# Forming the gate's rows inside the middle pass instead of ahead of the experts, and a loop for masked attention

## The reference, cut to what matters

```python
x = x + _L0_attn_ref(_layernorm(x), ...)          # self-attention, 16 heads
x = x + _L0_xattn_ref(_layernorm(x), ctx, ctx, ...)   # cross-attention, 64 keys a sequence
x = x + _L0_ffn_ref(_layernorm(x), ...)           # two matrices a sequence, no nonlinearity
x = x + _L1_attn_ref(_layernorm(x), ...)          # 8 experts, top 2 of a gate
x = x + _L1_xattn_ref(_layernorm(x), ctx, ctx, mask, ...)  # masked cross-attention
x = x + _L1_ffn_ref(_layernorm(x), ...)           # quantised feed-forward
# in _L1_attn_ref, the gate:
xn = rmsnorm(xf, gate_norm_w, 1e-6)
xn = rmsnorm(xn, norm_w, 1e-8)                    # inside bitlinear
xq = act_quant(xn)      # round(x * 127 / max|x| of the row) * max|x| / 127
wq = weight_quant(w)    # -1, 0 or 1, times mean|w|
gate_logits = xq @ wq.T # 4096 tokens x 8 experts
probs = softmax(gate_logits); topw, topi = top_k(probs, 2)
# then each expert takes the first 512 tokens that chose it
```

## Time and profile before

| | us |
|---|---|
| median of 3 runs (2372.21 to 2380.17) | 2373.59 |
| the profiled execution | 2368.86 |
| its span, first to last instruction | 2367.1 |
| span: load and self-attention | 1097.8 |
| span: middle, early part and loop | 272.3 |
| span: gate's rows and logits | 113.1 |
| span: routing, then scatter | 21.3 and 98.5 |
| span: experts | 220.0 |
| span: masked attention and the start of the last block | 382.0 |

### The profile page before, as it was taken

How to read it: one execution, slowest core, us unless ns; L and a number is a source line. 1 busy time by engine, 2 the same in 40 slices (tenths; PEclk the granted TensorE clock), 3 DMA queues, 4 the chain that set the end, 5 groups by cost and what they waited for, 6 DMA issues and landing times. The chain is left out here.

```text
span 2367.1 us, 42843 instructions
## 1 busy us (share of the span) xinstructions
PE 1715.8 (72%) x13321; PEld 1084.2 (46%) x13338; DVE 1550.3 (65%) x3111; ACT 1394.6 (59%) x2215; POOL 788.3 (33%) x749
## 2 busy tenths in 40 slices
PE   3789998989999898985888802122443788888577
PEld 1455555555555555553666601121222355555323
DVE  6877777777777777775233386744774675755775
ACT  3889888898979898991444412443553332323745
POOL 0534545454545455450000050470001444443000
PEclk9999999999999999996789955555766787878699
DMA  5222222222222222222122111332102201111001
GB/s 180 61 53 62 59 55 64 61 53 62 62 50 64 59 64 53 64 46 97 36 72 72 36 76 53 122 109 89 54 27 70 81 25 30 23 32 18 1 10 63
DMA packets 173822, 140.04 MB, mean 59 GB/s; under 512 B 83794, under 2 KB 155399, under 8 KB 173366
## 3 DMA queue, kind: packets, MB, share of 16 engines
q1 hardware_dynamic: 166710, 122.78, 19.4%
q0 software_dynamic: 6912, 14.71, 2.7%
HBM read 61.92 MB, written 20.97 MB: 35 GB/s over the span
## 5 line engine op out<-in xcount | busy, mean ns | idle before, releaser
L577 ACT ACTIVATE a_p_hi<-ps,a_probs_up,a_s_scale 128x512 f16<-128x512 f32 x512 | 397.7, 777 | 54.9 <-ACTq L575 54.1
L689 DVE TENSOR_REDUCE a_top<-ps 128x2 f32<-128x1024 f32 x256 | 313.1, 1223 | 132.6 <-DVEq L688 132.6
L578 ACT ACTIVATE a_probs<-ps,a_probs_up,a_s_scale 128x512 f32<-128x512 f32 x512 | 398.5, 778 | 0.0
L917 POOL TENSOR_TENSOR a_p_lo<-a_probs,a_p_hi 128x1024 f16<-128x1024 f32 x128 | 277.8, 2170 | 210.4 <-POOLq L916 169.1
L905 POOL TENSOR_TENSOR a_ops<-a_ident_down,a_top 64x256 f16<-64x256 f32 x256 | 158.9, 621 | 340.8 <-POOLq L900 332.3
L698 DVE TENSOR_TENSOR a_p_lo<-a_probs,a_p_hi 128x1024 f16<-128x1024 f32 x128 | 182.7, 1427 | 41.2 <-DVEq L697 41.2
L441 PE MATMUL ps<-a_ops 128*128 128x512 f16 x512 | 195.8, 382 | 17.7 <-PEq L439 17.6
L460 PE MATMUL ps<-a_v_hi,a_p_hi 128*128 128x65 f16 x2048 | 205.6, 197 | 2.1 <-PEq L455 2.0
L463 PE MATMUL ps<-a_v_lo,a_p_hi 128*128 128x64 f16 x2048 | 205.6, 195 | 0.0
L464 PE MATMUL ps<-a_v_hi,a_p_lo 128*128 128x65 f16 x2048 | 205.5, 196 | 0.0
L460 PEld LDWEIGHTS ps<-a_v_hi,a_p_hi 128*128 128x128 f16 x2048 | 191.2, 99 | 23.0 <-issue 11.1
(11 more groups left out here) (487 smaller groups left out, 3767.3 us busy)
## 6 DMA issues: line engine op xcount, KB each, us to landing
a_ops<-a_qk SPq DMA_DIRECT2D x384, 128.0 KB, 2.3
f_w<-in_L_ffn_W_dram SPq DMA_DIRECT2D x16, 1024.0 KB, 7.6
a_qd<-a_qk SPq DMA_DIRECT2D x128, 64.0 KB, 2.2
g_a<-in_L_attn_gp_w_dram SPq DMA_DIRECT2D x8, 1024.0 KB
X<-in_x_dram SPq DMA_DIRECT2D x8, 512.0 KB, 9.9
expert_in<-g_w SPq DMA_DIRECT2D x8, 512.0 KB
g_a<-in_L_attn_dp_w_dram SPq DMA_DIRECT2D x8, 512.0 KB
e_x_in<-expert_in SPq DMA_DIRECT2D x8, 512.0 KB, 4.3
```

The costliest lines, as they stand in the source:

```text
L577: nc.scalar.activation(p_hi[:, h % 2, k, :], scores, ACT.Exp, bias=probs_up[:], scale=s_scale[:])
L578: nc.scalar.activation(probs[:, h % 2, k, :], scores, ACT.Exp, bias=probs_up[:], scale=s_scale[:]).then_inc(st_taken, 1)
L689: nc.vector.tensor_reduce(top[:, c % 2, 2 * pair:2 * pair + 2], ps[:, ROW:ROW + 2, :], AX.X, ALU.max).then_inc(row_taken, 1)
L917: nc.gpsimd.tensor_tensor(p_lo[:, h % 2, 2:KT, :], probs[:, h % 2, 2:KT, :], p_hi[:, h % 2, 2:KT, :], ALU.subtract).then_inc(p_made_pool, 1)
```

## The change

The gate moves into the middle block. Its work on a sequence is cut into steps which follow the sequence's last addition by a fixed number of passes (NORMS 1, ROWS 2, SQUARES 3, QUANTISE 4, GATES 5), so the loop runs over b = 0..12. The small aggregates, inverse roots, `v`, `a`, `peak` stay on VectorE, but for four tiles at a time; the Newton steps go to GpSimd, except for the last sequence. `u` goes from GpSimd to ScalarE as one activation with a scale and a shift; the rounding to `r` goes from VectorE to ScalarE. The gate's weights are loaded and rounded in the early part of middle. Two `f_rows` are moved ahead of `scores` on TensorE, and ahead of the last two `w2_out` on ScalarE. The experts' first block begins with the softmax; its staging memory for weights is a tile of its own, so the loads no longer wait. In masked_attention the seven written-out passes become a hardware loop.

```diff
-        for b in range(B + 1):
+        for b in range(B + GATE_STEPS):
             if b < B:
                 in_order += [("pT", b), ("w2T", b, 0), ("w2T", b, 1)]
+            if 1 <= b <= B:
+                in_order += [("f_rows", b - 1, 0), ("f_rows", b - 1, 1)]
+            if 0 <= b - GATES < B:
+                in_order += [("gates", b - GATES)]
             if b + 1 < B:
                 in_order += [("scores", b + 1)]
...
+            if 0 <= b - QUANTISE < B:
+                in_order += [("gate_rows", b - QUANTISE)]
...
+                def newton(root, half, tmp, ready, done):
+                    pool.wait_ge(ready, 1)
+                    pool.sem_inc(ready, -1)
+                    for _ in range(3):
+                        nc.gpsimd.tensor_tensor(tmp, root, root, ALU.mult)
+                        pool.drain()
+                        nc.gpsimd.tensor_tensor(tmp, tmp, half, ALU.mult)
+                        pool.drain()
+                        nc.gpsimd.tensor_scalar(tmp, tmp, 1.5, None, ALU.add)
+                        pool.drain()
+                        nc.gpsimd.tensor_tensor(root, tmp, root, ALU.mult)
+                        pool.drain()
+                    pool.drain().then_inc(done, 1)
...
+                    if 0 <= b - SQUARES < LAST:
+                        newton(again_root[:], again_half[:], again_tmp[:], seeded_again, rooted_again)
+                    if 0 <= b - NORMS < LAST:
+                        newton(first_root[:], first_half[:], first_tmp[:], seeded, rooted)
...
+                def experts_rows(b):
+                    act.wait_ge(u_ready, 1)
+                    act.sem_inc(u_ready, -1)
+                    for t in range(TT):
+                        n = b * TT + t
+                        nc.scalar.activation(gate.u[:, n, :], X[:, n, :], ACT.Identity, scale=u_factor[:, t:t + 1], bias=u_shift[:, t:t + 1])
+                    act.wait_ge(v_made, 1)
+                    act.sem_inc(v_made, -1)
+                    for t in range(TT):
+                        nc.scalar.activation(g_junk[:, t * D:(t + 1) * D], g_v[:, t, :], ACT.Square, accum_out=squares[:, t:t + 1])
+                    act.drain().then_inc(squared, 1)
...
+                    for t in range(TT):
+                        nc.scalar.activation(a[:, t, :], a[:, t, :], ACT.Identity, scale=per[:, b % 2, t:t + 1], bias=up[:])
+                    act.drain()
+                    nc.scalar.activation(g_r[:].rearrange("p t d -> p (t d)"), a.rearrange("p t d -> p (t d)"), ACT.Identity,
+                                         bias=minus_up[:])
...
+                    if 0 <= b - GATES < B:
+                        gate_logits(b - GATES)
+                    if 0 <= b - SQUARES < B:
+                        gate_squares(b - SQUARES)
+                    if 0 <= b - ROWS < B:
+                        gate_values(b - ROWS)
+                    if 1 <= b <= B:
                         add_outputs(b - 1)
+                    if 0 <= b - NORMS < B:
+                        gate_norms(b - NORMS)
+                    if 0 <= b - SQUARES < B:
+                        gate_steps(b - SQUARES)
...
-                for b in range(B - 1):
+                with pe.Fori(0, B - 1) as b:
                     sequence(b, more=True)
```

More of the change, by code:

```diff
@@ L1275, in turn_back, with gate_rows, gates @@
                     last.then_inc(back_full, 1)
+                def gate_rows(b):
+                    bank = bank_of["gate_rows", b]
+                    pe.wait_ge(r_made, 1)
+                    pe.sem_inc(r_made, -1)
+                    take(bank)
+                    for t in range(TT):
+                        for c in range(DC):
+                            at = (t * DC + c) * P
+                            last = nc.tensor.transpose(ps16(bank)[:, at:at + P], g_r[:, t, c * P:(c + 1) * P], ident16[:])
+                    last.then_inc(r_turned, 1)
+                def gates(b):
+                    bank = bank_of["gates", b]
+                    pe.wait_ge(r_out, 1)
+                    pe.sem_inc(r_out, -1)
+                    take(bank)
+                    for t in range(TT):
+                        for c in range(DC):
+                            last = nc.tensor.matmul(ps[:, bank, t * E:(t + 1) * E], g_rT[:, t, c, :], gwT[:, c, :],
+                                                    start=(c == 0), stop=(c == DC - 1))
+                    last.then_inc(gates_full, 1)
                 for bank in range(BANKS):
@@ L1289, in _ @@
                                     ident[0:B * DC, 0:B * DC]).then_inc(cols_full, 1)
+                pe.wait_ge(gw_part, 1)
+                pe.sem_inc(gw_part, -1)
+                take(early_bank["gw"])
+                nc.tensor.matmul(ps[:, early_bank["gw"], 0:1], ones[:], gw_sum[:], start=True, stop=True).then_inc(gw_total, 1)
                 over.turn(pe, peak[:])
@@ L1329, in _ @@
                 last.then_inc(pre_full, 1)
+                pe.wait_ge(gw_round, 1)
+                pe.sem_inc(gw_round, -1)
+                take(early_bank["gwT"])
+                for c in range(DC):
+                    last = nc.tensor.transpose(ps[:, early_bank["gwT"], c * E:(c + 1) * E], gw[:, c * P:(c + 1) * P], ident[0:E, 0:E])
+                last.then_inc(gw_turned, 1)
                 for c in range(DC):
@@ L1344, in _ @@
                         turn_w2(b, 1)
+                    if 1 <= b <= B:
+                        for c in range(DC):
+                            f_rows(b - 1, c)
+                    if 0 <= b - GATES < B:
+                        gates(b - GATES)
                     if b + 1 < B:
@@ new lines, in gate_logits @@
+                def gate_logits(b):
+                    bank, seq = bank_of["gates", b], slice(b * TT, (b + 1) * TT)
+                    dve.wait_ge(gates_full, 1)
+                    dve.sem_inc(gates_full, -1)
+                    nc.vector.scalar_tensor_tensor(out=gate.logits[:, seq, :], in0=ps[:, bank, 0:TT * E].rearrange("p (t e) -> p t e", e=E),
+                                                   scalar=gw_mean[:], in1=g_step[:, seq].unsqueeze(2).broadcast_to([P, TT, E]),
+                                                   op0=ALU.mult, op1=ALU.mult).then_inc(free[bank], 1)
@@ L2718, in _ @@
                 power(0)
-                for b in range(B - 1):
+                with act.Fori(0, B - 1) as b:
                     sequence(more=True)
@@ L2808, in _ @@
                 maximum(0, 1)
-                for b in range(B - 1):
+                with dve.Fori(0, B - 1) as b:
                     sequence(b, more=True)
```

393 lines of the change are left out of this document (199 added, 194 removed).

## The result

The changed kernel takes 2308.03 us, the median of 4 runs (2299.66 to 2309.09), against 2372.9 us (4 runs, 2361.68 to 2380.17). The ratio is 0.9723, 95% interval 0.9678 to 0.9768: 65 us less, where 53 were forecast (2321 us, range 2298 to 2352).

| stage | before | after | difference | forecast |
|---|---|---|---|---|
| start of middle to the first `f_both` of `pair_turned` 1 | 73.5 | 76.7 | +3.2 | +1 |
| from there to the end of the last `f_outT` | 194.8 | 222.5 | +27.7 | +21 |
| last `f_outT` to the softmax | 117.1 | 35.5 | -81.6 | -78 |
| softmax to scatter | 21.3 | 21.8 | +0.5 | 0 |
| scatter | 98.4 | 102.9 | +4.5 | 0 |

A forecast was written before the change was run, and what follows sets the result against it. A VectorE chain before the softmax and, in middle's loop, ScalarE's first half plus TensorE's second were taken as the bound; -110.5 + 21 + 32.5 + 1 + 3 = -53 us gave 2321 us, range 2298 to 2352.

The forecast's parts named there:

- Removed: 110.5: Between middle's end and the softmax: of 113.2 us of VectorE's chain, 2.7 remain, so 110.5 us go.
- +32.5: Tail after the last `f_outT`: ScalarE's roundings, copies and squares, then logits, take 36.4 us instead of 3.9.
- The loop: Middle's passes: ScalarE's added work, less the moved `w2_out`, plus a clock loss in pass 8, costs 21 us.
- the same clock loss then falls on `scores` rather than on `outputs`, and I count no second one: Passes 5 to 7: TensorE waits about 3 us at `gates`; the clock loss only moves, adding nothing.
- The early part: Start of middle: the gate's loads, one reduction and one matmul join a chain, costing 1 us.
- The scatter: GpSimd's 64 indirect DMAs after the routing: unchanged at about 98 us, the fills having landed.
- Masked attention: The seven passes as a loop: branches and address registers cost 3 us, within 0 to 8.
- The same instructions and waits: Masked attention as a loop: nothing changes but a branch and address registers per pass, 3 us in all.
- the one in which `outputs` runs at full clock: Middle's loop: ScalarE's half shortens or TensorE's full clock regains the loss, hiding the 21 us; 2300 us, chance 0.13.
- fetches in the masked loop: Masked attention: each pass stops at its branch for a fetch, 28 us in seven passes; 2346 us, chance 0.06.
- GpSimd slowing VectorE: Gate work in middle: GpSimd's newtons hold VectorE up, 70 us or more beyond the forecast; 2391 us, chance 0.04.
- a factor of 2.2, not 2.7: VectorE's pass in middle: stretching the gate's 10 us decides the time from a factor of about 2.7 on.

The follow-up runs named there:

- Experiment 4: The changed kernel with the gate's eight small matmuls moved behind the last two turns of `w2` on TensorE: 2298.1 us, ratio 0.968 to the kernel before.
- experiment 5: Traces compared after one 2.06 us wait (pass 1 of 24.1 or 32.0 us); also the kernel before with only `f_rows` moved early: 2364.87 us.
- `before_rows`: The kernel before with only the two `f_rows` moved ahead of `scores` on TensorE and the last two `w2_out` on ScalarE: 2364.87 us, ratio 0.9966.
- Experiments 1 to 3: Masked passes looped on all engines (2355.87 us), TensorE (2371.66) or VectorE (2351.57), or given memsets (2357.35, 2357.84), against the kernel before; changed kernel unlooped: 2310.54.
- experiment 6: The changed kernel with the gate's matmuls behind the last `w2` turns and `u` formed by GpSimd instead of ScalarE: 2280.63 us, ratio 0.9602.

## Why the prediction was right, and where it was not

**The gate's chain.** "Removed: 110.5" and the tail's "+32.5" make -78.0; measured -81.6. The 2.8 us from the logits to the softmax were forecast as 2.7. From the last `f_outT` to the logits' end it took 32.7 us, not 36.4: the copy and its waits are 2.5 us a sequence, not 2.9, a rounding 3.5 with its waits, not 3.7, and `gate_u` with the squares 3.9, not 4.4. That ScalarE is what the tail waits for holds.

**The loop.** Forecast +21, measured +27.7. Passes 3 and 4 cost 2.6 and 3.7 us (forecast 2.8), pass 7 3.7 (forecast 4), pass 8 6.5 (forecast 7). Passes 1 and 2 gained 3.4 and 2.8 us instead of 1.6. Passes 5 and 6 are what was off: +9.1 and +8.4 instead of +4. The step that failed is "the same clock loss then falls on `scores` rather than on `outputs`, and I count no second one". It fell on both, and on `w2` and the values, so that TensorE came 5.1 us late for `outputs` in pass 5. Experiment 4 shows it: with only the values behind the wait, passes 5 and 6 cost 3.9 and 4.7 us. My mistake was to price a wait by its length and not by what is queued behind it at half clock. The length tells little here: in pass 6 TensorE waited 1.62 us at `f_rows` and only 0.96 at `gates`, the clock fell all the same while `scores` ran (near 1329.3), and `outputs` came 3.7 us late.

**The early part.** Forecast +1, measured +3.2 in the profiled execution. In the seven kernels that have the changed early part it took 76.7 and 76.9 us in two executions and 72.8 to 73.1 in five, and before it was 73.5. The two long ones are those in which TensorE's clock stayed at half there (experiment 5). So the +3.2 goes with the clock, and the forecast term is too small to be seen beside it.

**The scatter.** Forecast unchanged, measured +4.5 (102.9 us). It did not wait for the fills: SP issued the last of them at 1440.2, and the scatter began at 1454.4. About half of the 4.5 is the execution that it is compared with: the seven kernels that have the scatter of the kernel before took 98.4 to 101.4 us, 100.1 in the mean, the seven with the changed one 100.7 to 103.3, 102.1 in the mean. GpSimd's indirect DMA takes 0.97 us alone and up to 2.95 beside a rounding of VectorE. GpSimd's timeline of the changed kernel, and VectorE's:

```profile
1461.33 0.97 POOL L2064 DMA_INDIRECT expert_in<-gate_u,m_slot  x1 [0.30 <-issue]
1462.61 2.04 POOL L2064 DMA_INDIRECT expert_in<-gate_u,m_slot  x1 [0.31 <-issue]
1464.95 2.90 POOL L2064 DMA_INDIRECT expert_in<-gate_u,m_slot  x1 [0.30 <-issue]
```

```profile
1462.51 1.95 DVE L2232 TENSOR_SCALAR g_stage<-g_stage,g_minus_half_w 128x2048 bf16<-128x2048 f32 x2
1464.65 3.55 DVE L2238 SCALAR_TENSOR_TENSOR g_w<-g_stage,g_half_w 128x2048 bf16<-128x2048 f32 x2 [0.19 <-DVEq L2236]
```

Each slow DMA (over 1.2 us) has such a partner in both kernels, but for the first of the changed one. Before, 16 of the 64 were slow and lost 16.3 us over 0.97 each; after, 17, and 21.3. The rounding is the same work (48.12 and 48.45 us in the stage); how the two sequences of instructions fall on each other would then set the loss. This is read from the traces and was not tried. The Trainium skill (GPSIMD Engine Reference, section Specifications) lists GpSimd's SBUF interfaces as shared with VectorE, with contention where a VectorE instruction has two SBUF inputs. The second rounding instruction (`g_w<-g_stage`) has two, and beside it the DMAs took 1.93 to 2.95 us, so the trace agrees; of a DMA's issue the section says nothing.

**Masked attention.** Forecast +3, measured -22.7. "The same instructions and waits" was true of the instructions, and the price of 3 us for branches was not found: with the loop on TensorE alone the stage took 376.5 us, against 374.2 and 376.2 written out (`before_rows`). With the loop on VectorE its first instruction after a wait for scores starts 0.11 to 0.15 us later. What failed is the silent step that equal instructions have equal durations. Experiments 1 to 3 show that a shift of 0.04 to 0.21 us on VectorE, by its loop or by a useless memset, takes away a clock drop of some 10 us in most passes. Why the clock falls at one phase and not at the other stays open. The loop is worth 15.5 us on the kernel before. How much of the changed kernel's gain is the loop's is not settled: with its passes written out its masked attention took 357.5 us, between the two lengths, and the whole could not be told from the changed kernel's.

The mismatches cancel in part: loop +7, early part +2, scatter +4.5 and two small ones on one side; masked attention 26, the tail 4 and the last block 2 on the other. That the whole came out so near is partly luck: without masked attention the profiled gain would be 47 us, where 56 were forecast for the rest, and the 23 us that brought it up come from a clock drop that the prediction did not know of. Of the rivals, the one in which `outputs` runs at full clock happened in passes 1 and 2; "fetches in the masked loop" did not. GpSimd slowing VectorE did not happen with the newtons, which touch 4 or 12 values (they took 4.3 and 5.4 us in pass 5, and the 32 instructions of `gate_v` 0.47 to 0.50 us each), and did with `u`, in experiment 6. One figure of that rival is wrong by its own terms: 9 + 10 us times the factor reaches a pass of 31 us at a factor of 2.2, not 2.7.

## What to carry to other kernels

Price a wait on TensorE by all that is queued behind it, at both clocks, and put small matmuls with a late input where little stands between them and the next wait. When a stage that the change hardly touches moves by per cents, compare the granted clock of one pass before looking for a cause in the code, and shift the stage by 0.1 us with a useless instruction to tell chance from cause. Work that leaves the engine which ends the waits can come back in full: `u` was 2.07 us a pass and a wait, and six passes gave 14 us. Where the work goes must be looked at too: in the tail it gave nothing.

## What the runs showed of the hardware that was not expected

The same code with the same 2.06 us wait ran the next 16 us at a granted clock of 1.00 in one execution and 0.51 in another; what differed was the clock 20 us earlier (0.50 against 0.93 over 4 us). A memset of 0.11 us, four times a pass, which made the next instruction end 0.04 us later, went with masked attention 22 us shorter in the profile (374.2 to 352.0) and a kernel 0.6% faster. VectorE's steps over 4 numbers took 1.63 and 1.75 us instead of 0.16 beside GpSimd's 128x1024 subtraction and product. GpSimd's issue of an indirect DMA took up to 2.95 us instead of 0.97 beside VectorE's 128x2048 rounding to bf16.
